# Self attention of a diffusion block: scores computed a second time with keys in the rows instead of transposing probabilities, and a new order of the projections

## The reference

```python
shift_a, scale_a, gate_a, shift_m, scale_m, gate_m = jnp.split(silu(c) @ W_mod + b_mod, 6, axis=-1)
q, k, v = jnp.split((_ln(x) * (1 + scale_a) + shift_a) @ W_qkv + b_qkv, 3, axis=-1)      # per head
attn_out = softmax(q k^T * hd ** -0.5) v
x = x + gate_a * (attn_out @ W_proj + b_proj)
c_attn_out = softmax(q_c k_c^T * hd ** -0.5) v_c      # q_c from _ln(x) @ W_qc, k_c, v_c from _ln(context) @ W_kvc
x = x + c_attn_out @ W_cproj + b_cproj
x = x + gate_m * mlp(_ln(x) * (1 + scale_m) + shift_m)
```

## Time and profile before

| | |
|---|---|
| median of 3 runs | 3096.2 us (3096.01 to 3103.77) |
| profiled execution, its own time | 3103.15 us |
| span in the profile | 3101.4 us |
| TensorE busy over the span | 2780.5 us, 90% |
| VectorE, ScalarE, GpSimd | 58%, 40%, 36% |

### The profile page before, as it was taken

The page is one execution under the profiler, slowest core; times in us unless marked ns, Lnnn a source line. Parts: engine busy times, 40 slices in busy tenths (PEclk is TensorE's granted clock), DMA queues, the critical chain, the costliest instruction groups (busy, mean ns, idle before and its releaser), DMA issues. The chain is left out here.

```text
span 3101.4 us, 50821 instructions
## 1 busy us (share of the span) xinstructions
PE 2780.5 (90%) x18688; PEld 2231.1 (72%) x18688; DVE 1810.1 (58%) x3450; ACT 1226.8 (40%) x2979; POOL 1105.1 (36%) x1191
## 2 busy tenths in 40 slices
PE   3899999999962699999999999999955999999998
PEld 1688887888751577777777777777634888888886
DVE  2466767667633377777777777776735444444431
ACT  2455655565531144444444444444433221222110
POOL 0021212112110066666666666666751022202211
PEclk8899999999975899999999999999966999999999
DMA  5333444444313333333333433433313111111110
GB/s 168 93 93 103 108 110 115 108 109 105 92 43 97 80 93 105 104 105 106 103 105 104 106 101 104 107 105 83 96 59 112 35 38 48 47 33 43 43 45 21
DMA packets 169756, 269.39 MB, mean 87 GB/s; under 512 B 28839, under 2 KB 84647, under 8 KB 169495
## 3 DMA queue, kind: packets, MB, share of 16 engines
q1 hardware_dynamic: 166439, 258.80, 30.8%
q0 software_dynamic: 3072, 7.34, 0.7%
HBM read 111.04 MB, written 36.77 MB: 48 GB/s over the span
## 5 line engine op out<-in xcount | busy, mean ns | idle before, releaser
L1345 ACT ACTIVATE cross_prT<-cross_tr_ps 125x448 f32<-125x448 f32 x768 | 404.9, 542 | 361.4 <-PE cross_tr_ps L1143 349.0
L1243 DVE TENSOR_REDUCE cross_nmax<-cross_sc_ps 112x1 f32<-112x750 f32 x512 | 459.2, 928 | 37.9 <-PE cross_sc_ps L1126 37.6
L1390 POOL TENSOR_TENSOR cross_part<-cross_prT 125x448 f32<-125x448 f32 x256 | 293.5, 1147 | 340.6 <-PE cross_or_ps L1163 226.5
L1143 PE MATMUL cross_tr_ps<-cross_qst,cross_kst 98*125 98x224 f32 x1536 | 310.4, 287 | 26.1 <-DVE cross_cT_l L1226 22.3
L1143 PEld LDWEIGHTS cross_tr_ps<-cross_qst,cross_kst 98*125 98x125 f32 x1536 | 243.3, 189 | 101.4 <-issue 46.0
L1126 PE MATMUL cross_sc_ps<-cross_kst,cross_qst 96*112 96x500 f32 (+1 forms) x1024 | 281.3, 357 | 25.8 <-DVE cross_nmax L1243 11.7
L1392 POOL TENSOR_TENSOR cross_part<-cross_part,cross_prT 125x448 f32<-125x448 f32 x256 | 294.3, 1150 | 20.1
L756 ACT ACTIVATE self_pr<-self_sc_ps,self_nmax 112x224 f32<-112x224 f32 x512 | 224.7, 444 | 179.0 <-DVE self_nmax L640 176.6
L1773 ACT ACTIVATE mlp_hv<-mlp_h_ps,mlp_b 128x512 f32<-128x512 f32 x112 | 77.2, 689 | 521.8 <-PE mlp_h_ps L70 507.9
L640 DVE TENSOR_REDUCE self_nmax<-self_sc_ps 112x2 f32<-112x448 f32 x256 | 159.1, 622 | 160.3 <-PE self_sc_ps L444 159.4
L1700 DVE CAST mlp_hT_h<-mlp_hv 128x512 fp32r<-128x512 f32 x112 | 53.5, 478 | 323.7 <-ACT mlp_hv L1773 323.7
(11 more groups left out here) (176 smaller groups left out, 6776.2 us busy)
## 6 DMA issues: line engine op xcount, KB each, us to landing
cross_kst<-cross_nat_h SPq DMA_DIRECT2D x512, 93.8 KB, 2.2
cross_kst<-cross_nat_l SPq DMA_DIRECT2D x256, 93.8 KB, 2.2
cross_c_in<-in_context SPq DMA_DIRECT2D x90, 250.0 KB
cross_qst<-qc SPq DMA_DIRECT2D x192, 112.0 KB, 2.5
self_kst<-self_nat_h SPq DMA_DIRECT2D x128, 112.0 KB, 2.3
self_qst<-self_natq_h SPq DMA_DIRECT2D x128, 112.0 KB, 2.3
mlp_x<-in_w_mlp SPq DMA_DIRECT2D x32, 256.0 KB
self_x_in<-in_x SPq DMA_DIRECT2D x16, 448.0 KB, 6.4
```

Of the source, the lines that this page charges most:

```text
L1143: last = pe.matmul(bank(step, c)[0:SN, m * N:(m + 1) * N], kst[:, g, j, kt * SN:(kt + 1) * SN], qst[:, g, j, :], start=True, stop=True)
L1243: dve.tensor_reduce(nmax[:, g % 2, t, j:j + 1], sc_ps[t][0:QN, SC0:SC0 + S], AX_X, ALU.max, negate=True).then_inc(maxed, 1)
L1345: act.activation(prT[:, slot(h), 2 * c:2 * c + 2], bank((h + LAG) % NH, c)[0:SN, 0:2 * N].rearrange("p (k t) -> p k t", k=2), ACT.Exp).the ...
L1390: pool.tensor_tensor(part[:], prT[:, j, 0:2], prT[:, j, 2:4], ALU.add).then_inc(pre_summed, 1)
```

## The change

Only the self phase changes (and `select` goes from the constants). The probabilities are no longer transposed. Instead the scores are computed twice: first as before, only for the row maxima; then (`score_t`) with the keys in the rows, which gives them transposed, as `pv` wants them. Since the maximum now belongs to a column, it can't be a bias: it is subtracted in the matmul by two more rows of the contraction (98 instead of 96), ones in `kst` and the negated maximum, as high and low part, in `qst`. For that, per group of four heads: VectorE splits the maxima, TensorE transposes them, VectorE copies them to `mrow`, and a DMA on SP's queue places them in `qst`. ScalarE computes one exponential of 112 x 448 per head, straight into `prT`. GpSimd adds the two key tiles (`sum_p`), `sums` multiplies with ones, which puts the sum of each head in all 32 rows of it, and `normalize` takes the reciprocal of 128 x 224. The second scores, exponentials, sums and products with v run six heads behind the first scores (`LAG`), so those of the last heads lie in the next pass. `FILL` has a new order, c has its own tiles `natc`, one half of v belongs to b itself, ty to b-2, and there are B + 2 passes.

The new order, banks and lag:

```diff
+        FILL = [[("v", 1, 0)], [("v", 1, 1)], [("ty", 0, 0)], [("k", 0, 0), ("k", 0, 1)],
+                [("k", 1, 0), ("ty", 1, 0)], [("k", 1, 1), ("c", 0, 0)], [("c", 0, 1)], [("q", 0, 0), ("c", 1, 0)],
+                [("c", 1, 1), ("q", 0, 1)], [("q", 1, 0), ("q", 1, 1)], [("p", 0, 0)], [("p", 0, 1), ("p", 1, 0)],
+                [("p", 1, 1), ("tx", 0, 0)], [("v", 0, 0), ("tx", 1, 0)], [("v", 0, 1)], []]
+        BANKS = [f for step in FILL for f in step if f[0][0] != "t" and f[2] == 0]
+
+        def of(f):
+
+            return 0 if f[0:2] == ("v", 1) else {"k": 1, "q": 1, "v": 1, "p": -1, "c": -2, "tx": 2, "ty": -2}[f[0]]
...
-        FILL = [[("tx1", 1, 0), ("c", 0, 0), ("c", 0, 1)], [("c", 1, 0)], [("c", 1, 1)], [("k", 0, 0), ("k", 0, 1)],
-                [("k", 1, 0)], [("k", 1, 1)], [("p", 0, 0), ("p", 0, 1)], [("p", 1, 0)],
-                [("p", 1, 1), ("q", 0, 0)], [("q", 0, 1)], [("q", 1, 0)], [("q", 1, 1), ("v", 0, 0)],
-                [("v", 0, 1)], [("ty", 0, 0), ("v", 1, 0)], [("ty", 1, 0), ("v", 1, 1)], [("tx0", 0, 0)]]
...
+        def late(b, h, att, prv):
+            if h >= LAG:
+                return [(b, h - LAG)] if att else []
+            return [(b.plus(-1), h - LAG + NH)] if prv else []
...
+        def late_group(b, h, att, prv):
+
+            if h % HPG != (LAG + HPG) % HPG:
+                return []
+            g = (h - LAG - HPG) // HPG
+            if g >= 0:
+                return [(b, g)] if att else []
+            return [(b.plus(-1), g + KC)] if prv else []
```

SP's list of a pass, and TensorE's new parts:

```diff
             def body(b, att, nxt, prv, old):
-                a, z = b.plus(1), b.plus(-1)
+                a, z, y2 = b.plus(1), b.plus(-1), b.plus(-2)
+                if far(b):
+                    load_x(b.plus(2))
+                if att:
+                    place_maxima(b, 0)
                 if prv:
                     load_res(z)
-                if far(b):
-                    load_x(b.plus(2))
+                if nxt:
+                    stack(a, k_l, nat, kst, k_stacked, (0, 1, 0), range(0, 2))
+                if att:
+                    place_maxima(b, 1)
+                if nxt:
+                    stack(a, k_l, nat, kst, k_stacked, (0, 1, 0), range(2, HPG))
                 if old:
-                    store_qc(b.plus(-2))
+                    store_qc(y2)
                 if nxt:
-                    stack(a, k_l, nat, kst, k_stacked, (0, 1, 0))
+                    stack(a, q_l, natq, qst, q_stacked, (0, 0, 1), range(0, 2))
+                if att:
+                    place_maxima(b, 2)
+                if nxt:
+                    stack(a, q_l, natq, qst, q_stacked, (0, 0, 1), range(2, HPG))
                 if prv:
                     store_x1(z)
-                if nxt:
-                    stack(a, q_l, natq, qst, q_stacked, (0, 0, 1))
+                if att:
+                    place_maxima(b, 3)
...
+            def turn_maxima(b, g, prv, old):
+
+                pe.wait_ge(m_l, b.n(KC, g + 1))
+                if g == 0 and old:
+                    pe.wait_ge(yT_l, b.plus(-2).n(2, 1))
...
+                for t in range(QT):
+                    last = pe.transpose(tx_ps[0:2 * HPG, t * QN:(t + 1) * QN], nsplit[:, g % 2, t].rearrange("p s j -> p (s j)").bitcast(F32),
...
+                last.then_inc(m_ps, 1)
+
+            def score_t(b, h):
+                g, j = h // HPG, h % HPG
+                if j == 0:
+                    pe.wait_ge(m_in, b.n(16 * KC, 16 * (g + 1)))
...
+                wait(pe, exped, b.n(NH, h - 1))
...
+                    last = pe.matmul(st_ps[h % 2][0:QN, kt * N:(kt + 1) * N], kst[:, b.par, j, g, kt * QN:(kt + 1) * QN],
+                                     qst[:, b.par, j, g, :], start=True, stop=True)
+                last.then_inc(turned, 1)
...
+                pe.wait_ge(exped, b.n(NH, HPG * g + HPG))
...
-                pe.wait_ge(inverted, b.n(KC, g + 1))
-                for t in range(QT):
-                    last = pe.transpose(or_ps[0:HPG, R0 + t * QN:R0 + (t + 1) * QN], rinv[:, :, t], ident[0:QN, 0:QN])
-                last.then_inc(rT_ps, 1)
-
...
+            def sums(b, g):
+                pe.wait_ge(p_summed, b.n(NH, HPG * (g + 1)))
+                for j in range(HPG):
+                    last = pe.matmul(or_ps[HD * j:HD * j + HD, R0:R0 + N], ones[:], psum[:, slot(g * HPG + j)], start=True, stop=True)
+                last.then_inc(sum_ps, 1)
...
+            def fill(b, kind, c, part, o):
+                if part == 0:
+                    wait(pe, *bank_free(b, kind, c))
...
+                    pe.wait_ge(xT_l, o.n(1, 1))
                     channels(c, part, wqkv, KC + 2 * c, xT, k_ps)
...
+                    pe.wait_ge(oT_l, o.n(KC, KC))
...
+            def turn_x(b, c, o):
+
+                if c == 1:
+                    pe.wait_ge(xT_v, o.n(2, 1))
...
+            def turn_y(b, c, o, att):
+                if c == 0:
+                    pe.wait_ge(m_row, o.n(KC, 2 * KC) if o.c + 1 < B else o.n(KC, KC))
+                elif att:
+                    pe.wait_ge(m_row, b.n(KC, 1))
+                else:
...
                 for h in range(NH):
-                    if h == 1 and prv:
-                        pv(z, KC - 1)
-                    if h % HPG == 1 and h > 1 and att:
-                        pv(b, h // HPG - 1)
-                    if h > 0 and att:
-                        trans_p(b, h - 1)
-                    if h == 0 and prv:
-                        trans_p(z, NH - 1)
-                    for kind, c, part, o in fills(b, h, nxt, prv, old):
-                        fill(kind, c, part, o, b, att, nxt, prv, old)
-                    if h == 2 and prv:
-                        spread(z, KC - 1)
-                    if h % HPG == 2 and h > 2 and att:
-                        spread(b, h // HPG - 1)
+                    for o, l in late(b, h, att, prv):
+                        score_t(o, l)
+                    if h % HPG == HPG - 1 and att:
+                        turn_maxima(b, h // HPG, prv, old)
+                    work = fills(b, h, "kqvpc")
+                    for f in work[0:1]:
+                        fill(b, *f)
                     if h < NH - 1 and att:
                         score(b, h + 1)
                     if h == NH - 1 and nxt:
-                        score(a, 0)
...
+                        score(b.plus(1), 0)
+                    for f in work[1:]:
+                        fill(b, *f)
+                    for o, g in late_group(b, h, att, prv):
+                        pv(o, g)
+                    for o, g in late_group(b, h - 1, att, prv):
+                        sums(o, g)
+                    for _, c, _, o in fills(b, h, ("tx",)):
+                        turn_x(b, c, o)
+                    for _, c, _, o in fills(b, h, ("ty",)):
+                        turn_y(b, c, o, att)
```

VectorE:

```diff
+            def split_maxima(b, g):
+                dve.wait_ge(maxed, b.n(NH, HPG * (g + 1)))
+                wait(dve, m_ps, b.n(KC, g - 1))
+                dve.tensor_copy(nsplit[:, g % 2, :, 0], nmax[:, g % 2]).then_inc(m_h, 1)
+                dve.wait_ge(m_h, b.n(KC, g + 1))
+                dve.tensor_tensor(nsplit[:, g % 2, :, 1], nmax[:, g % 2], nsplit[:, g % 2, :, 0].bitcast(F32), ALU.subtract).then_inc(m_l, 1)
...
+            def copy_maxima(b, g):
+                dve.wait_ge(m_ps, b.n(KC, g + 1))
+                wait(dve, m_in, b.n(16 * KC, 16 * g))
+                dve.tensor_copy(mrow[:], tx_ps[0:2 * HPG, 0:N]).then_inc(m_row, 1)
...
-                dve.wait_ge(rb_done, b.n(KC, g + 1))
+                dve.wait_ge(sum_ps, b.n(KC, g + 1))
+                wait(dve, o_done, b.n(KC, g))
+                dve.reciprocal(rb[:], or_ps[:, R0:R0 + N]).then_inc(inverted, 1)
...
+                dve.wait_ge(inverted, b.n(KC, g + 1))
                 dve.tensor_tensor(ou[:, g], or_ps[:, 0:N], rb[:], ALU.mult).then_inc(o_done, 1)
...
+                    if h % HPG == HPG - 1 and att:
+                        copy_maxima(b, h // HPG)
+                    for o, g in late_group(b, h - 2, att, prv):
+                        normalize(o, g)
                     if h < NH - 1 and att:
                         row_max(b, h + 1)
                     if h == NH - 1 and nxt:
...
+                        row_max(b.plus(1), 0)
+                    if h % HPG == HPG - 2 and att:
+                        split_maxima(b, h // HPG)
+                    for f in fills(b, h, "kqcp"):
+                        evict(*f)
+                    for _, c, _, o in fills(b, h, ("tx",)):
+                        modulate(o, c)
+                    for _, c, _, o in fills(b, h, ("ty",)):
+                        low_y(o, c)
+                    if h == 9 and prv:
+                        low_o(z)
...
-                    if prv and h == 10:
+                    if prv and h == 15:
                         stats(z, y, summed, lambda t: z.n(2, t + 1), st2, mv2, stats2, mvs2)
-                    if prv and h == 11:
```

(57 more changed lines are left out.)

406 lines of the change are left out of this document (153 added, 253 removed).

## The result

The changed kernel takes 3207.5 us (median; 3199.4 to 3210.2) against 3097.0 us before on the same chip: ratio 1.035, 95% interval 1.032 to 1.037. The profiled execution of it took 3206.9 us, its span is 3204.7 us, 103.3 more than before.

The account below looks back on a forecast made before the run. TensorE's instruction stream was taken as the bound. 42.3 + 4.9 + 3.4 + 2.0 + 4.0 = 56.6 us per pass against 49.7, +97 over 14 passes, with edges -8 and +6, gave 3190 us, range 3105 to 3240.

Parts of the forecast that it names:

- work: TensorE's work per pass: 45.3 less 6.4 for transposes of probabilities plus 3.4 for second scores, 42.3 us.
- gap A: Steps 1 to 3: first k projection waits for the low half of xT behind a ScalarE, TensorE, GpSimd chain, 4.9 us.
- gap B: Steps 9 and 10: output projection waits for VectorE's low halves of o, behind q's low halves, 3.4 us.
- small waits: At turns of the maxima, before c, before q and before the second turn of x: together 2.0 us, bounds 0 and 3.0.
- clock: TensorE's granted clock falls to 1.2 GHz after each of the two gaps: 4.0 us per pass, bounds 0 and 6.8.
- the sign: First k projection of a pass waits for GpSimd's low half of xT, 4 to 5.5 us in all behind the product with v.
- 45.3: TensorE's work per pass before the change: period 49.7 less 2.0 seam waits, 1.7 clock and 0.7 other idle, in us.
- the exchanges per group of heads: Inverse transposes and spreading matmul go, maxima transposes and sums by ones come: taken as even, bounds -1.8 and 1.4.
- Edges: Outside the full passes: first pass -8 us (-12 to 0), last two stretches +6 us (0 to +12).
- (1): Rival: gaps are there, but the clock falls once and small waits drown in slack; 52.6 us per pass, 3135 us; chance 0.2.
- (2): Rival: faster, xT cast early enough; 47.5 us per pass, 3063 us, deciding from A + B = 3.5 us; chance 0.14.
- (3): Rival: GpSimd's sums hold VectorE up, 4 us more per pass, 60.6 us, 3247 us; chance 0.12.

Follow-up runs that it names:

- experiment 7: Kernel of experiment 6 with VectorE instead of GpSimd subtracting the low half of xT, at the end of step 1: 3066.1 us, ratio 0.990.
- experiment 4: Changed kernel with xT cast directly behind the copy of v and the low halves of o ahead of q's low halves: 3106.9 us, ratio 1.002.
- experiment 6: Kernel of experiment 4 with the first half of k moved to step 2 and the first turn of y to step 3: 3098.9 us, ratio 1.000.
- experiment 8: Kernel of experiment 7 with the first half of c one step later, both halves of chunk 0 at step 6: 3061.4 us, ratio 0.988.
- experiment 2: Changed kernel with ScalarE casting xT directly behind the copy of v and GpSimd subtracting at step 1: 3164.2 us, ratio 1.022.

## Why the prediction was right

The verdict, the place and the size came as forecast: 3190 against 3207. The experiments show the two chains as the cause. The size owes something to luck, since the errors of the terms partly cancel. Step by step, per pass, by the yardstick of experiment 7:

| | forecast | measured |
|---|---|---|
| work | 42.3 | 44.9 |
| gap A | 4.9 | 3.8 |
| gap B | 3.4 | 3.5 |
| small waits | 2.0 | 1.2 |
| clock | 4.0 | 4.6 |
| sum | 56.6 | 58.0 |

Work and clock were put 3.2 us too low, gap A and the small waits 1.9 too high.

**Gaps.** Both were found from the written order and the durations of the earlier trace rows. B came at its forecast (3.45 in the timeline), and its chain is the one named: q's low halves, then the four of o. VectorE took 1.94 us for these instead of 1.53, since sums of GpSimd ran beside them. A's chain was right too (layer norm, turn, cast, subtraction), but the profile counts only 3.8 us of it as idle, under the 4 to 5.5 that I had named as the sign. From start to start gap A measures about 0.6 + 1.45 + 2.2 = 4.25; the ends of the matmuls before the waits, 0.1 to 0.2 us each, are counted as busy.

**Work: the term that was most off.** 42.3 was forecast and 44.9 measured. Half of this is the starting figure. 45.3 took 1.7 us of clock out of every pass, but the two seams of the earlier trace rows do not stand for all: of the thirteen passes of the earlier trace rows six have no fall of the clock. Two neighbours:

```profile
499.30:549.40 50.10, 48.49 (x387) 40.76 (x386) 34.13 (x76) 28.98 (x100) 8.96 (x9) 0.97 0.41 107
549.40:597.80 48.40, 46.80 (x386) 39.07 (x385) 34.12 (x76) 28.90 (x99) 8.96 (x9) 1.00 0.42 110
```

The six are busy 46.6 to 46.8 us, so the work before was 46.7. The mean pass lost 1.1 us to the clock and 1.9 to waits, where I had taken 1.7 and 2.7.

The other half is the change itself: 45.3 - 6.4 + 3.4 promised 3.0 us less work, and it is 46.7 - 44.9 = 1.8. In passes without a fall, from start to start and with the idle time taken out, the transposes of probabilities and the projection matmuls behind them give back 5.5 + 0.7 = 6.2 us, near the 6.4. The term that failed is the second scores: 4.8 us, 0.30 a pair, not 3.4. (The remaining 0.4 come from the exchanges per group of heads, taken as even, and from the transposes of x and y.) The 0.21 of the earlier trace rows is a pair's price ahead of transposes. Ahead of projections, in the changed kernel (timeline of TensorE, inside a step):

```profile
506.62 0.58 PE L536 MATMUL self_or_ps<-self_psum,self_ones 112*32 112x224 f32 x8
507.14 0.47 PE L516 MATMUL self_st_ps<-self_qst,self_kst 98*112 98x224 f32 x2
507.44 0.28 PE L68 MATMUL self_pj_ps<-self_yT_l,self_wqc_h 128*128 128x224 f32 x1
...
510.33 0.37 PE L516 MATMUL self_st_ps<-self_qst,self_kst 98*112 98x224 f32 x2
510.66 0.37 PE L68 MATMUL self_pj_ps<-self_xT_l,self_wqkv_h 128*128 128x224 f32 x1
510.87 0.28 PE L69 MATMUL self_pj_ps<-self_xT_h,self_wqkv_l 128*128 128x224 f32 x1
```

The pairs take 0.30 and 0.33, and behind the second the projection matmul takes 0.21 instead of 0.11, as it did behind transposes. Sums by ones (0.52 for eight matmuls) came near the 0.45.

**Clock.** 4.0 forecast, 4.6 measured, by a fall behind each gap, as said. The Trainium skill, "TensorE: Matmul & The Clock Gate", section "HAM oscillation — how this bites in real kernels", describes a loop that pays for the clock in every turn. The changed kernel agrees, with both falls in each of twelve passes; the kernel before and those of experiments 4 and 6 do not, with a fall in only 7 of 13, 9 of 11 and 7 of 11. The reasoning by gap failed in the experiments: closing B took 1.9 off the clock's share and closing A's longest wait 1.8, while both together took 3.1, and closing or filling B lengthened the fall behind A.

**Small waits.** 1.2 of 2.0: before c, before q and at one turn of the maxima, 0.3 to 0.4 each, and 0.25 before the scores, which I had not named. The second turn of x, priced at 0.65, did not wait, nor did two of the three turns of the maxima. The maxima's DMA never showed.

**The passes and the edges.** That 14 times +6.9 = +97 came so near the +100.4 is luck: the first full pass has no y to turn behind its cast and no c, gap A is 2.0 us in it and no fall follows, and it takes 50.0 us, about as before; the twelve behind it take 58.0, 8.3 more instead of 6.9. The two errors nearly cancel. Edges: -4.6 and +7.5 where -8 and +6 stood.

**Rivals.** (1), a single fall of the clock and no small waits, is out: 4.6 and 1.2. (2), faster because the cast is early enough, is out for this order, but experiments 7 and 8 are that case, made: with idle 2.6 to 2.9 and no fall a pass takes 47.5 to 47.8. That it meets the 47.5 worked out there is luck, since the work is 44.9 and not 42.3 and no fall is left. The point from which it was to decide, A + B = 3.5 us, was too high: in experiment 4 they are 2.9 and a pass takes 50.5, more than the 49.7 before. (3) is part of the truth, at 1.7 us per pass. That the second scores themselves would be the cause is excluded by experiments 7 and 8, which have them all and beat the kernel before.

What stays open: which pass has a fall, and how long it lasts. Behind A, with waits of 1.0 and 1.2 us, experiment 2 has none and experiment 4 has one in nine passes of eleven. The idle time of a pass does not decide it either: experiments 7 and 8 have no fall with 2.9 and 2.6 us, the kernel before has some with 1.9. A rule that gives the falls from the waits I have not found.

## What to carry to other kernels

When a change takes work off the bounding engine and reorders the lists, write the order down step by step and time each chain against what the engine has to do meanwhile: here 1.8 us of work were won per pass and 10.1 us of waits and clock lost (13.1 against 3.0), two places in the lists held 101 of the 110 us, and with the order mended the same idea is 1.2% faster than before. Price an added instruction by its distance in the place where it will stand, between the neighbours that it will have, and take the clock's loss from all passes and not from two. A move into an empty step only moves the wait; fill the step with work that needs nothing late.
